# A decoder layer on one core: the attention stage with eight batches in flight, written order per engine, and GpSimd taking SBUF-only steps

## The reference

```python
# 1: differential self attention, 16 heads of 16, in two halves of 8
qkv = x @ w_qkv.T; q, k, v = split(qkv)
q, k = apply_rope(q), apply_rope(k)
scores = einsum(q_half, k_half) * 16 ** -0.5 + triu(ones, k=1)   # adds 1, doesn't mask out
out = softmax(scores1) @ v - lam * softmax(scores2) @ v
y = out.transpose(0, 2, 1, 3).reshape(b, e, s)      # then normalised per group of heads
y = ((y - mean_g) * rsqrt(var_g + 1e-5)) * gamma + beta
x = layernorm(x + (0.2 * y).reshape(b, s, e) @ wo.T)
# 2: cross attention without projections: 32 query heads of 8, 8 key heads; keys = values = ctx
x = layernorm(x + softmax(x_heads @ ctx_heads.T / sqrt(8)) @ ctx_heads)
# 3: experts: 2 shared and the best 2 of 8 by sigmoid(x @ w_router.T), each silu(gate) * up, down
x = layernorm(x + experts(x))
```

## Time and profile before

| | |
|---|---|
| median of three runs | 1021.01 us (1017.29 to 1021.79) |
| the profiled execution | 1024.9 us, span 1023.1 us |
| mean granted TensorE clock | 0.853 |
| TensorE busy | 875.6 us, 86% of the span |
| VectorE, ScalarE, GpSimd busy | 651.1, 514.2, 216.8 us |
| DMA | 53.07 MB, mean 52 GB/s |

### The profile page before, as it was taken

How to read it: one execution, slowest core, us unless ns; L and a number is a source line. 1 busy time by engine, 2 the same in 40 slices (tenths; PEclk the granted TensorE clock), 3 DMA queues, 4 the chain that set the end, 5 groups by cost and what they waited for, 6 DMA issues and landing times. The chain is left out here.

```text
span 1023.1 us, 19465 instructions
## 1 busy us (share of the span) xinstructions
PE 875.6 (86%) x7471; PEld 550.8 (54%) x7471; DVE 651.1 (64%) x1476; ACT 514.2 (50%) x941; POOL 216.8 (21%) x321
## 2 busy tenths in 40 slices
PE   3877889998899888998966787999999999999970
PEld 1444455545545455455543354556557788887760
DVE  2358677657866577577773288767766666665643
ACT  3444566645655455556544235434535555555543
POOL 3112212122211221122110006800001232323234
PEclk9657799857878578777785699999999999999995
DMA  7190000000000000000000115714222333232325
GB/s 215 57 251 14 7 7 6 7 2 6 7 6 7 1 6 6 6 2 1 2 1 1 60 37 185 235 67 148 78 68 47 49 45 50 45 51 42 49 32 169
DMA packets 40552, 53.07 MB, mean 52 GB/s; under 512 B 9488, under 2 KB 35344, under 8 KB 40464
## 3 DMA queue, kind: packets, MB, share of 16 engines
q1 hardware_dynamic: 33312, 42.49, 14.2%
q0 software_dynamic: 7152, 9.34, 5.6%
HBM read 33.14 MB, written 18.68 MB: 51 GB/s over the span
## 5 line engine op out<-in xcount | busy, mean ns | idle before, releaser
L1483 PE MATMUL ps<-wr,xr_hi 128*128 x624 | 129.3, 299 | 0.0
L575 DVE TENSOR_REDUCE c_qs<-ps 128x4 f16<-128x512 f32 x128 | 82.4, 689 | 71.6 <-PE ps L808 71.3
L1185 POOL DMA_INDIRECT acc<-y_sb,xin x39 | 60.8, 1559 | 269.9 <-ACT y_sb L1253 266.9
L575 DVE TENSOR_REDUCE a_qs<-ps 128x4 f16<-128x512 f32 x128 | 83.6, 690 | 41.2 <-PE ps L808 41.2
L1483 PE MATMUL ps<-xg_hi,wsh 128*128 128x512 f16 x320 | 103.6, 386 | 5.8 <-DVE xg_lo L1360 5.8
L445 ACT ACTIVATE a_pt<-ps 128x512 f32<-128x512 f32 x128 | 75.3, 600 | 48.2 <-PE ps L833 47.0
L1224 ACT ACTIVATE th<-ps 128x384 f32<-128x384 f32 (+1 forms) x118 | 57.3, 486 | 81.8 <-PE ps L1483 81.7
L1483 PE MATMUL ps<-wr,xr_lo 128*128 x312 | 93.4, 299 | 0.0
L445 ACT ACTIVATE c_pt<-ps 128x512 f32<-128x512 f32 x128 | 70.0, 600 | 44.9 <-PE ps L833 44.9
L1367 DVE SCALAR_TENSOR_TENSOR th<-th,ps 128x384 f32<-128x384 f32 (+1 forms) x118 | 65.1, 551 | 34.5 <-ACT th L1224 34.3
L1229 ACT ACTIVATE hs<-th 128x384 f16<-128x384 f32 x78 | 36.6, 470 | 78.7 <-DVE th L1370 78.7
(11 more groups left out here) (214 smaller groups left out, 1822.7 us busy)
## 6 DMA issues: line engine op xcount, KB each, us to landing
wst<-in_wx SPq DMA_DIRECT2D x30, 640.0 KB, 4.2
xs<-zero SPq DMA_DIRECT2D x1, 5031.0 KB, 20.4
xin<-xs SPq DMA_DIRECT2D x39, 129.0 KB, 2.1
a_x<-in_x SPq DMA_DIRECT2D x16, 128.0 KB, 2.1
x_row<-in_x SPq DMA_DIRECT2D x1, 2048.0 KB, 10.6
acc<-x_row SPq DMA_DIRECT2D x4, 512.0 KB, 5.8
x_row<-acc SPq DMA_DIRECT2D x8, 256.0 KB, 4.6
out<-x_row SPq DMA_DIRECT2D x8, 256.0 KB, 2.1
```

The source lines that it names most:

```text
L575: dve.tensor_reduce(qs[:, c:c + 4, f % 4, USED], t.sc[:, f % 2, :].rearrange("p (j n) -> p j n", j=4), AX.X, ALU.max, negate=True).then_in ...
L1185: pool.indirect_dma_start(acc, bass.IndirectOffsetOnAxis(ap=row, axis=0), y_sb[:, n % 2, :], None, compute_op=ALU.add).then_inc(f_acc, 16)
L1483: ins = pe.matmul(o, l[x], r[y], start=(first and n == 0), stop=(last and n == m - 1), skip_group_check=not (first and last))
```

## The change

The order of every engine in the attention block is written anew. `body(n)` now runs for n = 0 to 22 and works on up to eight batches: x of n, first pass of n-1, second pass and mix of n-2, group norm, out projection, layer norm and cross stacks of n-3, both cross passes of n-4 (two fills of the first pass already in the iteration before), cross residual of n-5, norm and transposes for the router of n-6, router of n-7. No step is added to or taken from the arithmetic, apart from the forms that follow.

- Score banks go by reader: 0 and 1 for the passes that VectorE reads (A and C in turn), 2 and 3 for those that ScalarE reads. The waits come from a table `RINGS`: for each ring of banks the uses in order, from which `Turns` derives whose reading a use waits for.
- GpSimd takes from VectorE: the subtraction of the two softmaxes, the group norm's scale and bias and its application, both layer norms, the cross residual addition.
- Copies change hands: `qm` of A and `qt` of C go to VectorE, `qm` of C and `qt` of A to ScalarE.
- `x` is loaded once, in three transfers, into `x_all`, and transposed from there.
- More intermediate tiles (`yn`, `y2`, `bn2`, `mv2`) and a semaphore per step in place of counted steps.

```diff
+RINGS = (
+    (2, (("cm", 4, 2), ("cm", 4, 3), ("cm", 4, 4), ("cm", 4, 5), ("cm", 4, 6), ("cm", 4, 7), ("am", 1, 0),
...
+    (1, (("aqT", 1, 0), ("akT", 1, 0), ("v", 1, 0), ("xT", 0, 0), ("qk", 0, 0), ("are", 1, 0))),
+    (1, (("rt", 7, 0), ("cre", 4, 0), ("x2T", 6, 0), ("ckT", 3, 0), ("cqT", 3, 0))),
+    (1, (("apv0", 2, 0), ("abk0", 2, 0), ("cpv0", 4, 0), ("cbk0", 4, 0))),
...
+ITERATIONS = B + 7
...
+class Turns:
+    def __init__(self, rings, readers):
+        self.readers, self.at, self.last = readers, {}, {}
+        for size, names in rings:
+            order = [(x, n - s, f) for n in range(ITERATIONS) for x, s, f in names if 0 <= n - s < B]
+            for i, key in enumerate(order):
+                self.at[key] = i
+                self.last[key] = order[i - size] if i >= size else None
...
+    def wait(self, pe, name, b, f=0):
+        key = self.last[name, b, f]
+        if key:
+            sem, per = self.readers[key[0]]
+            pe.wait_ge(sem, per * key[1] + (key[2] + 1 if per == FILLS else per))
...
-            t.sc = ps[:, bank:bank + 2, :]
+        def score_bank(t, kind, b, f):
+            name = ("a" if t is A else "c") + kind
+            return ps[:, (0 if kind == "m" else 2) + turns.place(name, b, f) % 2, :]
...
-            sp.dma_start(A.x[:], a["x"][0:P, :]).then_inc(s_xb, 16)
+            sp.dma_start(x_all[:, 0:1, :], xv[:, 0:1, :]).then_inc(s_x[0], 16)
...
+            sp.dma_start(x_all[:, 1:4, :], xv[:, 1:4, :]).then_inc(s_x[1], 16)
...
+            def mix_sub(b):
+                pool.wait_ge(A.s_mix, 2 * b + 2)
+                if b:
+                    pool.wait_ge(A.s_yn, 2 * b)
+                pool.tensor_tensor(A.y[:], A.t1[:], A.t2[:], ALU.subtract).then_inc(A.s_y, 1)
+            def group_scale(b):
+                n = 5 * b
+                pool.wait_ge(A.s_g2, b + 1)
+                pool.tensor_tensor(A.gw[:, 0:1], A.g2[:, 0:1], A.g2[:, 0:1], ALU.mult).then_inc(A.s_gp, 1)
...
+                pool.tensor_tensor(A.gbi[:], bet[:], A.gbi[:], ALU.subtract).then_inc(A.s_gs, 1)
+            def group_norm(b):
+                pool.wait_ge(A.s_gs, b + 1)
+                if b:
+                    pool.wait_ge(A.s_ynT, b)
+                for h in range(EC):
+                    c = slice(h * P, (h + 1) * P)
+                    pool.tensor_scalar(A.yn[:, c], A.y[:, c], A.gsc[:, h:h + 1], A.gbi[:, h:h + 1],
+                                       ALU.mult, ALU.add).then_inc(A.s_yn, 1)
+            def normalise(y, mv, t, b, ready):
+                pool.wait_ge(t.s_rstd_ok, b + 1)
+                pool.tensor_scalar(x_all[:, b, :], y[:], mv[:, 0:1], t.rstd[:, 0:1], ALU.subtract, ALU.mult
+                                   ).then_inc(ready, 1)
+            def cross_add(b):
+                pool.wait_ge(C.s_mix, 2 * b + 2)
+                if b:
+                    pool.wait_ge(x2_ready, b)
+                pool.tensor_tensor(C.y[:], C.t1[:], x_all[:, b, :], ALU.add).then_inc(C.s_y, 1)
+            def body(n):
+                if live(n - 3):
+                    group_norm(n - 3)
+                if live(n - 1):
+                    q_low(n - 1)
...
+                if live(n - 2):
+                    group_scale(n - 2)
+                if live(n):
+                    rope_sum(n)
```

1102 lines of the change are left out of this document (557 added, 545 removed).

## The result

The changed kernel takes 912.9 us (median of 4 runs, 909.0 to 915.9) where the kernel before takes 1021.4 (4 runs, 1017.3 to 1023.2) on the same chip: a ratio of 0.898, 95% interval 0.894 to 0.902. Forecast were 944 us, in a range of 905 to 1000. The range held the time; the forecast was 31 us too slow, and the rival "full" (908 us) came closest. The profiled execution took 912.3, its span is 910.0. The profile of the kernel before is of one of its longer executions (1024.9 us; the runs on record took 1003.3 to 1025.2, with medians of 1010 to 1021 from one group of runs to the next), so differences between the two profiles are somewhat larger than those between medians.

A forecast was written before the change was run, and what follows sets the result against it. TensorE's queue at a dropping clock was taken as the bound. Ten steady batches (-49 us), head (-4) and drain (-24) made -77: 948 us on the profiled execution's basis, 944 on the median's, range 905 to 1000.

The forecast's parts named there:

- rival "full": No thin stretch in the new order, TensorE stays at 2.4 GHz: 24.5 us a batch, 908 us in all; chance 0.19.
- What bounds: Attention stage: TensorE's queue at a clock that drops is what costs, 32.0 us per steady batch before.
- The share of the full level: Steady batches: TensorE's full clock taken for three quarters of the time, giving 27.1 us a batch; chance 0.50.
- a weak place: TensorE's 1.7 us wait before the restack of A, each batch, taken as a spot where the clock may drop.
- the two ends (24.5 and 29.5): Bounds for a steady batch in us: all at full clock, or the old clock shares of 0.56 full and 0.44 half.
- Work: TensorE's work per steady batch at full clock, counted from fills, stacks, values and projections: 21.9 us, against 22.8 before.
- Waits: TensorE's waits per steady batch: 2.6 us, 1.7 at the restack of A and 0.9 at the first cross values.
- the restack of A: It takes the bank that the rope reads, so TensorE waits 1.7 us for VectorE each batch.
- Head and drain: Attention before and behind the steady batches: head 131.3 less 4 us, drain 86 us against 110.2, so 24 less.
- The other queues: ScalarE 18.5, VectorE about 18, GpSimd some 11.5 us per batch: none reaches 21.9, so none bounds by its sum.
- A single price: GpSimd's steps taken from VectorE: 0.67 us assumed for each 256-wide operation.
- Experts: Stage after attention, 447.2 us, code the same in both versions; any other time was named a sign of being wrong.

The follow-up runs named there:

- e3: Kernel before plus sixteen full-row 512-column matmuls per batch, ahead of self-attention max fills and cross exp fills, output unchanged; ratio to before 1.013.
- e4: Changed kernel without the eight mask matmuls of a batch, so masked scores are not pushed down; ratio to before 0.897, batch 23.94 us.
- e8: Kernel before plus sixteen added full-row matmuls per batch at 256 columns each, output unchanged; ratio to before 1.007.
- e9: Kernel before plus 512-column full-row matmuls only ahead of the eight self-attention max fills, none ahead of cross exp fills; ratio to before 1.002.
- e10: Changed kernel with the eight mask matmuls replaced by 256-column ones that the fill overwrites, masked scores not pushed down; ratio to before 0.892.
- e1: Changed kernel with six wide SBUF-only steps (mix difference, group norm halves, layer-norm applications, cross addition) back on VectorE; ratio to before 0.920.

## Why the prediction was right, and where it was off

- **What bounds.** Right. TensorE's queue and its clock were read as the cost, and the account puts about 6 of 9.1 us on the clock. e3 and e4 show that full-row matmuls added or taken away move the level, up in the old order and down in the new. One reading of the rows was wrong without effect: TensorE's longest wait in the steady stretch of before isn't 1.2 us but 1.42 (at 436.20).
- **The share of the full level is the step that failed.** "I take the full level for three quarters of the time" gave 27.1 us; it was all of the time. 24.5 at the full level would have followed, 2.6 of the 4.2 us by which a batch was off. I had judged the 1.7 us of wait a weak place. The wait is there every batch (1.39) and the level holds, while e4's falls where TensorE waits for next to nothing. What I had no row for was how much is needed, and I split the difference; the two ends (24.5 and 29.5) were right to keep, and the likeliest was the end.
- **Work.** 21.9 forecast, 20.95 measured, 1.0 us less. The count of groups was right, but fills of two passes on different array rows overlap more than the pair that I had taken as the pattern (four in 0.36 us).
- **Waits.** 2.6 forecast, 1.93 measured. Right for the restack of A, its cause and nearly its size (1.7, measured 1.39). The cross values wait 0.17 instead of 0.9; a max fill waits 0.37 that I hadn't seen.
- **Head and drain.** -4 and -24 forecast, -4.9 and -24.9 measured (cut alike). The granted clock of a head is no measure: in the first body it reads 1.00 in one profile of the changed kernel and 0.61 in the other, with the same length, and a matmul of 512 columns takes 0.61 us in both, the half level's time (0.38 us at the full level).

```profile
14.23:31.89 17.66, 10.32 (x62) 5.40 (x62) 9.57 (x18) 3.14 (x6) 2.55 (x3) 1.00 0.45 127
27.68 0.61 PE L875 MATMUL ps<-wq_hi,a_xt_hi 128*128 128x512 f16 x1
```

```profile
14.03:31.68 17.65, 10.30 (x62) 5.41 (x62) 9.58 (x18) 3.14 (x6) 2.55 (x3) 0.61 0.45 130
27.49 0.61 PE L875 MATMUL ps<-wq_hi,a_xt_hi 128*128 128x512 f16 x1
```

  In the steady stretch the two agree: a mask takes 0.39 us where the clock reads 1.00 and 0.58 to 0.63 where it reads 0.50.

- **The other queues.** Right that none bounds by its sum: VectorE 18.0 us and GpSimd 12.0 per batch, about 18 and 11.5 forecast. A single price was wrong: 0.67 for each wide GpSimd operation, where a layer norm's application takes 1.24, and the group norm's two halves 0.88 together. No wait of another engine names these.
- **Experts.** "An experts' stage that is not 447 us" was named as a sign against me, and it was 455.5. It wasn't the change: the other profile of the same kernel shows 448.9, those of the experiments 444 to 453. Of the excess, 6.3 us differ between two executions of one kernel; where they come from inside the stage (a stretch of 40 us at a clock of 0.88 is shown above) wasn't settled.

In sum, from 948 on the profile's basis: the steady stretch -42 (27.1 to 22.89), head and drain -2, experts +8, which makes 912. That the range held is in part luck: without the 8 us of the experts, whose code is the same in both, the time would have come out at its lower edge, 905.

## What to carry to other kernels

When TensorE's granted clock in a stage is between its two levels, split the stage into waits, busy x clock, and busy x (1 - clock) before counting instructions: the last term may be the largest. Here an order that spreads the dense matmuls evenly removed it whole, not in proportion. Near the edge, taking TensorE work out can make a batch longer (e4: 1.05 us with 2.3 us less work, the total unchanged), so try a reduction with a look at the clock. Work added to hold the level shortened the steady batch in the profiles, and in no case the kernel (e3, e8, e9). Before you read a profile's difference as a gain, see how long its execution was beside the other runs of the same kernel, and check a granted clock against the duration of a matmul that you know. And once TensorE's queue is the path, a wait in it is worth filling only to the next bank that isn't free: four moves were worth 1.0 us of 1.9 us of waits.

## What the runs showed of the hardware

- The granted clock fell with TensorE busy 2.71 of 3.00 us (e4), and did not fall in 229 us with a wait of 1.4 us in every 22.9 (changed kernel). One fall cost 4.4 us (e10).
- At the start of a trace the granted clock can read 1.00 while matmuls take the half level's time (0.61 us for 512 columns, 0.38 at the full level).
- A layer norm's application ([128, 256], two per-partition scalars) takes 1.24 us on GpSimd, where its two-tensor operations of the same width take 0.67 to 0.74. The Trainium skill ("GPSIMD Engine Reference", 4.1 Engine selection) has two-input elementwise operations about twice as slow there as on VectorE, and one-input ones "roughly line-rate". The first fits roughly (0.67 to 0.74 against 0.43 on VectorE, 1.6 to 1.7 times); the second, if it means no such loss, doesn't fit this form (1.24 against 0.40).
- The same SBUF-only instruction on VectorE took longer while GpSimd worked on SBUF. The two halves of the group norm, alone in the kernel before, and in e1 beside the rope sum:

```profile
275.08 0.60 DVE L634 TENSOR_SCALAR a_t<-a_y,a_gsc,a_gbi 128x128 f32<-128x128 f32 x2
```

```profile
248.75 1.27 POOL L297 TENSOR_TENSOR a_rq<-a_rq,a_r 128x512 f32<-128x512 f32 x1
248.83 1.53 DVE L738 TENSOR_SCALAR a_yn<-a_y,a_gsc,a_gbi 128x128 f32<-128x128 f32 x2 [1.42 <-POOL a_gbi L350]
```

0.60 became 1.53 us, and GpSimd's own 1.27 stayed; the earlier trace rows show it once, 0.75 for L651 beside a GpSimd operation, where the same line took 0.40 with GpSimd idle. So where such a step meets a GpSimd one, moving it to GpSimd also frees VectorE of this tax, and e1's 2.8 us of work put back hold 0.9 of it.
